# AdaLN block on one core: the experts' first product from fp32r parts instead of f32

## The reference

```
h = layernorm(x) * (1 + ca) + sa
x = x + ga * attention(h)                     # 32 query heads, 8 key heads of 32
h = layernorm(x) * (1 + cb) + sb
logits = h @ router_w.T                       # 4 experts
gates  = softmax of the two largest logits
mid    = h @ A[e].T                           # 16 columns for each expert
x = x + gb * sum_e gates[e] * (mid[e] @ B[e].T) * 4
```

## Time and profile before

| | us |
|---|---|
| median of 3 runs | 3011.82 (3004.32 to 3011.96) |
| profiled execution, its own time | 3011.51 |
| its span, first to last instruction | 3009.7 |
| `project`, `attend`, `finish` (by the trace) | about 690, 1800, 520 |
| busy in the span: PE, DVE, ACT, POOL | 2894.5, 1931.0, 1526.7, 1798.2 |

### The profile page before, as it was taken

How to read it: one execution, slowest core, us unless ns; L and a number is a source line. 1 busy time by engine, 2 the same in 40 slices (tenths; PEclk the granted TensorE clock), 3 DMA queues, 4 the chain that set the end, 5 groups by cost and what they waited for, 6 DMA issues and landing times. The chain is left out here.

```text
span 3009.7 us, 49792 instructions
## 1 busy us (share of the span) xinstructions
PE 2894.5 (96%) x15590; PEld 1742.3 (58%) x15590; DVE 1931.0 (64%) x2572; ACT 1526.7 (51%) x2906; POOL 1798.2 (60%) x595
## 2 busy tenths in 40 slices
PE   6899999989999999999999999999999997999998
PEld 3687878874444444444444444444444435888886
DVE  3333333317777777777777777777777745766666
ACT  2111111105666666666666666666666662444444
POOL 2433333317888888888888888888888885211110
PEclk8899999998999999999999999999999998999998
DMA  6543334332211221221222122122212105333331
GB/s 229 172 137 124 129 131 137 129 116 84 56 45 43 55 51 36 55 51 42 49 51 52 39 51 55 39 48 55 51 36 55 41 12 165 96 110 107 108 105 63
DMA packets 156462, 241.61 MB, mean 80 GB/s; under 512 B 48992, under 2 KB 90400, under 8 KB 156320
## 3 DMA queue, kind: packets, MB, share of 16 engines
q1 hardware_dynamic: 156320, 240.05, 27.6%
HBM read 159.12 MB, written 79.82 MB: 79 GB/s over the span
## 5 line engine op out<-in xcount | busy, mean ns | idle before, releaser
L852 DVE TENSOR_REDUCE mx<-s_ps 128x1 f32<-128x1024 f32 x1024 | 1203.8, 1217 | 430.2 <-PE s_ps L921 423.5
L832 ACT ACTIVATE p_t<-st_ps 128x512 f32<-128x512 f32 x2048 | 1113.4, 595 | 553.3 <-PE st_ps L947 484.1
L790 POOL TENSOR_TENSOR p_sum<-p_sum,p_t 128x2048 f32<-128x2048 f32 x256 | 1173.3, 4583 | 22.1
L947 PE MATMUL st_ps<-q_st,k_st 98*128 98x512 f32 x2048 | 809.2, 435 | 11.3 <-ACT p_t L832 8.3
L947 PEld LDWEIGHTS st_ps<-q_st,k_st 98*128 98x128 f32 x2048 | 344.7, 187 | 604.3 <-ACT p_t L832 414.3
L921 PE MATMUL s_ps<-k_st,q_st 96*128 96x512 f32 x2048 | 657.9, 403 | 14.6 <-DMA q_st<-q_hi_d 10.9
L961 PE MATMUL num_ps<-p_t,v_sb 128*32 128x512 f32 x4096 | 546.1, 605 | 0.9 <-ACT p_t L832 0.9
L790 POOL TENSOR_TENSOR p_sum<-p_t 128x2048 f32<-128x2048 f32 x64 | 293.4, 4584 | 294.6 <-ACT p_t L832 294.6
L921 PEld LDWEIGHTS s_ps<-k_st,q_st 96*128 96x128 f32 x2048 | 389.6, 191 | 95.1 <-DVE mx L852 14.0
L372 POOL TENSOR_TENSOR o_lo<-side,o_hi 128x512 fp32r<-128x512 f32 x80 | 104.8, 1311 | 346.9 <-ACT o_hi L342 346.9
L1232 POOL TENSOR_TENSOR a_lo<-a_f,a_hi 128x1024 fp32r<-128x1024 f32 x32 | 76.1, 2379 | 358.9 <-ACT a_hi L1267 358.8
(11 more groups left out here) (129 smaller groups left out, 2820.0 us busy)
## 6 DMA issues: line engine op xcount, KB each, us to landing
q_st<-q_hi_d SPq DMA_DIRECT2D x128, 256.0 KB, 4.4
stage<-w_mod SPq DMA_DIRECT2D x48, 512.0 KB, 5.3
q_hi_d<-o_hi SPq DMA_DIRECT2D x64, 256.0 KB, 2.0
q_lo_d<-o_lo SPq DMA_DIRECT2D x64, 256.0 KB, 2.0
q_st<-q_lo_d SPq DMA_DIRECT2D x64, 256.0 KB, 4.1
att_d<-a_sb SPq DMA_DIRECT2D x128, 128.0 KB, 2.3
a_f<-att_d SPq DMA_DIRECT2D x32, 512.0 KB, 4.8
x_sb<-x SPq DMA_DIRECT2D x32, 512.0 KB, 5.4
```

Source lines behind the costliest of these rows:

```text
L790: nc.gpsimd.tensor_tensor(total, before, p_t[:, kt, :, :], ALU.add).then_inc(sum_done, 1)
L832: nc.scalar.activation(p_t[:, s, c, :], st_ps[:, c % 2, :], ACT.Exp, scale=SCALE)\
L852: nc.vector.tensor_reduce(mx[:, slot % 2, e:e + 1], s_ps[:, e % 2, :], AX_X, ALU.max)\
L947: nc.tensor.matmul(st_ps[:, c % 2, :], k_st[:, slot // 2, s * P:(s + 1) * P], q_st[:, slot, jj, h * QW:(h + 1) * QW], start=True, stop=True)\
```

## The change

- h is written once in f32 (`h_f`, one buffer in place of two). A new ACT instruction rounds it to fp32r as `h_hi`; a new POOL instruction computes `h_lo` = h_f - h_hi, and stands behind POOL's a_lo in the slot.
- `down` is loaded with 68 columns instead of 128; POOL splits it once, in slot 2, into `down_r` (high part in columns 0 to 67, low part in 68 to 135).
- The product is 16 fp32r matmuls: for each of eight k-steps one of `h_hi` by both parts (136 columns) and one of `h_lo` by the high part (68 columns, added to columns 0 to 67).
- DVE copies columns 68 to 135 of the product and adds columns 0 to 67 to them: one instruction more.
- On PE the product stands after the first six matmuls of the projection's second half (`BEFORE = 2`), not ahead of them, and the experts' first half directly behind the product.
- `h_lo` of a tile waits for the product of the tile before, and so does `h_hi`; the product waits for `h_lo_done`.

```diff
-        down = sb("down", [P, KT, P], F32)
+        down = sb("down", [P, KT, ER + E], F32)
...
-        h_t = sb("h_t", [P, 2, KT, P], F32)
+        h_f = sb("h2_f", [P, KT, P], F32)
+        h_hi = sb("h2_hi", [P, KT, P], F32R)
+        h_lo = sb("h2_lo", [P, KT, P], F32R)
+        down_r = sb("down_r", [P, KT, 2, ER + E], F32R)
...
-        BEFORE = 3
+        BEFORE = 2
...
-                        sp.dma_start(down[:, :, :], lora_in).then_inc(lora_loaded, 16)
+                        sp.dma_start(down[:, :, :], lora_in[:, :, 0:NM]).then_inc(lora_loaded, 16)
...
+                    now = tile_of(slot, b, t, 2)
+                    if now:
+                        T = now[0]
+                        pool.wait_ge(h_hi_done, T + 1)
+                        if not is_int(T, 0):
+
+                            pool.wait_ge(mid_ready, T)
+                        nc.gpsimd.tensor_tensor(h_lo[:, :, :], h_f[:, :, :], h_hi[:, :, :].bitcast(F32), ALU.subtract)\
+                          .then_inc(h_lo_done, 1)
                     if is_int(slot, 2):
 
                         pool.wait_ge(lora_loaded, LORA_LOADS)
+                        nc.gpsimd.tensor_copy(down_r[:, :, 0, :], down[:, :, :]).then_inc(down_step, 1)
+                        pool.wait_ge(down_step, 1)
+                        nc.gpsimd.tensor_tensor(down_r[:, :, 1, :], down[:, :, :],
+                                                down_r[:, :, 0, :].bitcast(F32), ALU.subtract).then_inc(down_step, 1)
...
                         act.wait_ge(turned, T + 1)
+                        if not is_int(T, 0):
+
+                            act.wait_ge(h_lo_done, T)
                         for kt in range(KT):
-                            last = nc.scalar.activation(h_t[:, tt % 2, kt, :], t_ps[:, kt * P:(kt + 1) * P],
+                            last = nc.scalar.activation(h_f[:, kt, :], t_ps[:, kt * P:(kt + 1) * P],
...
                         last.then_inc(h_ready, 1)
+                        act.wait_ge(h_ready, T + 1)
+                        if not is_int(T, 0):
+
+                            act.wait_ge(mid_ready, T)
+                        nc.scalar.copy(h_hi[:, :, :], h_f[:, :, :]).then_inc(h_hi_done, 1)
...
-                        step(nc.vector.tensor_copy(mid[:, :], g_ps[:, 0:ER + E]))
+                        step(nc.vector.tensor_copy(mid[:, :], g_ps[:, NM:2 * NM]))
+                        step(nc.vector.tensor_tensor(mid[:, :], g_ps[:, 0:NM], mid[:, :], ALU.add))
...
+                    if proj:
+                        project_half(proj, 1, range(BEFORE))
                     if mids:
-                        T, _, tt = mids
+                        T = mids[0]
                         if is_int(T, 0):
 
-                            pe.wait_ge(lora_loaded, LORA_LOADS)
-                        pe.wait_ge(h_ready, T + 1)
+                            pe.wait_ge(down_step, 2)
+                        pe.wait_ge(h_lo_done, T + 1)
...
                         for k in range(KT):
-                            last = nc.tensor.matmul(g_ps[:, 0:ER + E], h_t[:, tt % 2, k, :], down[:, k, 0:ER + E],
-                                                    start=k == 0, stop=k == KT - 1)
+                            nc.tensor.matmul(g_ps[:, 0:2 * NM], h_hi[:, k, :],
+                                             down_r[:, k, :, :].rearrange("p n c -> p (n c)"),
+                                             start=k == 0, stop=False)
+                            last = nc.tensor.matmul(g_ps[:, 0:NM], h_lo[:, k, :], down_r[:, k, 0, :],
+                                                    start=False, stop=k == KT - 1)
                         last.then_inc(mid_ready, 1)
-                    if proj:
-                        project_half(proj, 1, range(BEFORE))
```

More of the change, by code:

```diff
@@ L1104, in finish @@
         d_ps = ps("d_ps", [P, HW])
-        MID_T = slice(P, 2 * P)
+        MID_T = slice(2 * P, 3 * P)
+        NM = ER + E
         bo_in = sem("bo_in")
@@ L1129, in finish @@
         turned = sem("turned2")
+        down_step = sem("down_step")
         h_ready = sem("h2_ready")
+        h_hi_done = sem("h2_hi_done")
+        h_lo_done = sem("h2_lo_done")
         mid_ready = sem("mid_ready")
@@ L1367, in step @@
                             dve.wait_ge(r_step, T * STEPS + at[0])
-                        STEPS = 9
+                        STEPS = 10
                         dve.wait_ge(mid_ready, T + 1)
-                        step(nc.vector.tensor_copy(mid[:, :], g_ps[:, 0:ER + E]))
+                        step(nc.vector.tensor_copy(mid[:, :], g_ps[:, NM:2 * NM]))
+                        step(nc.vector.tensor_tensor(mid[:, :], g_ps[:, 0:NM], mid[:, :], ALU.add))
                         logit = mid[:, ER:ER + E]
```

## The result

The changed kernel takes 3080.99 us (median of 4 runs, 3071.62 to 3088.09), the kernel before 3011.03 (4 runs, 3004.32 to 3011.96): 1.0235 times as long, 95% interval 1.0204 to 1.0267. The forecast was 3065, range 3034 to 3084.

The account below looks back on a forecast made before the run. PE's order bounds the kernel (390.00 of 390.00 us busy mid-stage) unless the ACT-DVE chain is late, with 1.35 to spare. Slots 35.5, slot 32 0.4, start 4.8 and 6.0, drain 7.0 add 53.7 to 3011.51: 3065 us, range 3034 to 3084.

Parts of the forecast that it names:

- xn held to 0.55 behind POOL's end: Middle slots, DVE: xn waits for the end of POOL's a_lo (2749.83) and itself ends at 2750.38.
- PE waiting 1.4 ahead of the experts: Middle slots: PE waits for gmid_t's low part from 2749.90 to 2751.33, ahead of the experts' first half.
- a slot of 16.35: Slots 7 to 31: each takes 16.35 us, up by 1.42 from 14.93; 25 slots make 35.5.
- a later std: ACT in a slot: the cast of h_hi makes std 1.25 us late, ending at 2748.27; xn could start at 2748.51.
- Start: Stage's start: 4.8 for slot 4's projection waiting for a_lo, plus 6.0 for slots 4 to 6 at 2.0 each.
- drain: Slots 33 and 34: cast, subtraction and two waits with nothing beside them, 3.5 each, 7.0 us in all.
- slot 32: Slot 32 has no a_lo, so xn runs alone for 0.81; the slot grows by 0.4 us.
- The product: PE, each slot: 16 fp32r matmuls at 0.106 each, 1.70 us as before; bounds 0.75 and 3.4.
- if the clock fell from 2.4 to 1.2 GHz in each slot for nine matmuls: Rival, PE's clock behind the 1.4 wait: 53 us more, 3118; chance 0.09 shared with a dearer product, nearly all the product's.
- DVE's extra add: DVE, each slot: 68 columns, a quarter of a us, costed at nothing as covered by PE's 18 matmuls and transposes.
- the 53.7: Whole stage, sum of added us: 35.5 + 0.4 + 4.8 + 6.0 + 7.0.
- the upper bound of 3084: Whole kernel: top of the range, just above 3079, the rival with the product at its upper price of 3.4 us.

Follow-up runs that it names:

- experiment 3: The change with h_lo not computed on POOL, the product multiplying h_hi twice (h's low part missing); 3041.26 us, one run.
- experiment 4: The change without ACT's cast and POOL's subtraction: activations write h_hi directly, the product uses it twice; 3022.08 us, ratio 1.0053.
- experiment 6: The change with POOL's a_lo made to wait until DVE has written gmid_t's low part; 3042.35 us, one run.
- experiment 7: The change with POOL's a_lo made to wait for xn only, so a_lo starts ahead of gmid_t's low part; 3076.63 us, one run.
- experiment 9: The kernel before with only the change's PE order (BEFORE = 2: six matmuls, f32 product, experts); 3013.95 us, ratio 1.0010.
- experiment 8: The change with a_hi cast twice on ACT, 1.07 us more ahead of a_lo and std; 3098.81 us, one run.
- experiment 2: The change with the product back ahead of all nine projection matmuls, arithmetic kept; 3057.67 us, ratio 1.0171.
- experiment 1: The change with the experts' first half nine projection matmuls behind the product instead of directly behind it; 3040.42 us, ratio 1.0114.
- experiment 5: The change without DVE's added instruction (mid copied from columns 0 to 67 only, h_hi by down's low part missing); 3077.72 us, ratio 1.0231.
- 10: The change with experts nine matmuls later, down split ahead of the first h_lo, columns 68 to 135 copied by ACT; 3022.61 us, ratio 1.0036.

## Why the prediction was right, and where its sizes were off

**Right, by its own steps.** ACT's cast, a_lo behind h_lo, xn held to 0.55 behind POOL's end, gmid_t late, PE waiting 1.4 ahead of the experts, a slot of 16.35: measured are xn 1.93 and its end at 0.55, waits from 1.34 on, slots of 16.40. Experiments 3 and 4 take the two causes away one after the other and the slot goes to 15.6 and 14.89; 6 and 7 move DVE's wait to where the reading says that it must go. The Trainium skill (SBUF — State Buffer, Who interferes with whom) calls the port pair that DVE and POOL share an exclusive lock, held for the whole instruction; the runs agree, with 128x16 elements taking 1.89 and 64x128 elements 2.00 beside one POOL instruction. That the product waits for nothing, and that the move is free by itself, held too (experiment 9: 1.0010).

**The split of the slot's cost.** The prediction worked out 1.25 for a later std and then noted that a_lo's end overrides it. Experiment 8 shows how far that goes: 1.07 more on ACT cost 0.24. Without the subtraction too (experiment 3), xn ended 0.55 behind a_lo (2796.63 and 2796.08). So the cast matters to a slot by what it pushes back on POOL.

**Start, drain, slot 32.** 7.7 against 10.8 predicted; 6.1 against 7.0; -0.04 against +0.4. At the start POOL's tables began at 2537.15, behind h_lo and a split whose copy took 1.11 (I had 0.6) and whose subtraction 1.33 (1.3):

```profile
2532.21 2.39 POOL L1248 TENSOR_TENSOR h_lo<-h_f,h_hi 128x1024 fp32r<-128x1024 f32 x1 [12.61 <-ACT h_hi L1314]
2534.54 1.11 POOL L1253 CAST down_r<-down 128x544 fp32r<-128x544 f32 x1
2535.73 1.33 POOL L1255 TENSOR_TENSOR down_r<-down,down_r 128x544 fp32r<-128x544 f32 x1
2537.15 2.78 POOL L1257 TENSOR_SCALAR up_w<-up_w 128x1024 f32<-128x1024 f32 x1
```

That put the tables 12.3 later than before, counted from the stage's start (11.4 forecast), and slot 4's projection 5.4 (4.8). The three slots behind it, at 2.0 more each, were priced too dear: together they grew by 2.3 and not 6.0. In slot 32 the low part was ready in time.

**The product.** 1.71 was measured (2801.01 to 2802.64, plus 0.075 for the last) against 1.70 taken; inside an undisturbed slot the change from f32 is worth 0.04 to 0.05 (14.93 to 14.88 and 14.89). The 0.72 that was worked out from the Trainium skill (TensorE: Matmul & The Clock Gate, Back-to-back issue gap) is not seen: a matmul of 136 columns is followed after 0.146 and one of 68 after 0.075, each with its own weight load between.

**The term that was mis-sized: the clock.** The sum had nothing for it. It was a rival, "if the clock fell from 2.4 to 1.2 GHz in each slot for nine matmuls", at 2.1 per slot and 53 in all, and shared a chance of 0.09 "nearly all of it the product's", since 0.77 of idle had left it up and 4.86 had not the earlier trace rows, and 1.4 is nearer the first. The runs show something between: of the 25 slots it fell in 9 ordinary ones, for some seven matmuls, 1.5 a time, 13.9 in all, and at both of the loop's entries. Waits of 0.4 to 0.7 (experiments 2 and 3) did not bring it down; waits of 1.35 to 1.7 did in part of the slots.

**What the prediction did not have.** "DVE's extra add [...] I cost them at nothing, covered": its duration is covered, as predicted. But with one instruction more per slot in the loop's body, DVE starts late when the loop is entered again: in the change by 3.3 and 3.0 us against its other slots, measured from the transposes. The two slots cost 7.75 above ordinary ones here, clock included, and 12.8 in experiment 1. No term and no rival of the prediction had this.

These make the balance of the profiled execution against the 53.7: start 3.1, drain 0.9 and slot 32 0.4 less; 1.2 more for 25 slots at 16.40 instead of 16.35; 13.9, 7.75 and 1.1 more: 73.3, and with the 3.35 ahead of the stage 76.6. The difference of the medians is 70.

**What was luck.** A slot without a fall of the clock was forecast within 0.05 us, but the whole came out above the forecast, 19.6 in the profiled execution's stage and 16 by the medians: two costs that were not in the sum, 21.7 together, met only 4.4 of terms priced too dear. That 3081 still lies under the upper bound of 3084 is luck: the bound was set for a dearer product, and the product cost what was taken. One of the four runs, 3088.09, lies above it.

## What to carry to other kernels

When a kernel's bound engine is 100% busy and what it waits for comes only a us or so ahead of time, a step added to the engines that feed it is paid for as soon as it takes more than that margin. Count every instruction in front of the last one that the bound engine waits for, and those of POOL too where DVE, as here, waits for the end of POOL's. Ask also what the new arithmetic saves the bound engine: here it was 0.05 us of 14.93. Keep the consumer at a distance of some independent matmuls from what feeds it (experiment 1 against the change: some 40 us for nine matmuls between), since the idle time may also bring the clock down. And look at the first slot of each loop iteration apart from the others: one instruction more on an engine can cost there what it costs nowhere else.

## What the runs showed of the hardware beyond that

**A late start where the loop is entered again.** Over the ten experiments, the change and the kernel before, a wait of DVE's first instruction marked "issue" appears twice in the stage, 6.1 to 9.6 in total, in exactly those eight kernels in which DVE has the added instruction (the change, experiments 1 to 4 and 6 to 8), and in none of the four without (before, 5, 9, 10). From one entry to the next the trace has 378 records of DVE in each of those eight, and 362 in each of the four. The DMA queue q14, which carries instructions, goes with it: 104 or 105 packets in those eight, 94 or 95 in the four. The change and the kernel before, from section 3 of their pages:

```profile
q14 instruction: 104, 0.85, 0.1%
```

```profile
q14 instruction: 94, 0.77, 0.1%
```

In the stretch 2745 to 2762, where the late start of tile 14 lies, q14 has three packets, two of them between 2753 and 2757.7, while DVE stands idle; in the same stretch of experiment 5 it has none. That DVE waits for its own code, fetched again when the loop jumps back, is what these rows point to, but is not shown. Only the two lengths above were run, so from what length of a body on it happens stays open.

**The clock behind short waits.** In the change, waits of 1.34 to 1.50 left the clock up in some slots (2804.23) and waits of 1.36 to 1.56 brought it down in others, mostly every second or third slot. In experiment 7, with waits of 1.85 and more, it fell in 3 slots of 25, in experiment 8, with 1.58 to 1.74, in 14. So the length of the wait does not settle it; what does stays open.

**Pace of narrow fp32r matmuls.** With the clock down, as in the drain, a pair takes 0.42 (its first matmuls at 3057.15 and 3057.57), twice the 0.22 of the middle; f32 with 68 columns took 0.226 per record there, 0.45 for the two that make one k-step. The two forms of the product are equal in both states, within 0.03 per k-step.
